# A chunk's delta-rule solve in two halves of eight tokens, with TensorE's sums between them, and all output products on GpSimd

## The chip, the cores and the metric

The kernel runs on one core of a Trainium2 chip. The metric is device microseconds (us) of one execution. The trace is of one profiled execution, with the granted TensorE clock beside it (1.0 is 2.4 GHz, 0.5 is 1.2 GHz).

## The reference, cut to what matters

Two layers, each attention plus a feed-forward part, over x of [16 batches, 512 tokens, 256]. The change touches only the recurrence of layer 0's attention. There, with 16 heads and 64 x 64 states:

```python
q = silu(conv4(x @ Wq.T)); k = silu(conv4(x @ Wk.T)) * SCALE; v = silu(conv4(x @ Wv.T))
a = sigmoid(x @ Wa.T + ba); beta = sigmoid(x @ Wb.T + bb)
def step(S, inp):                 # one token, every batch and head
    qt, kt, vt, at, bt = inp
    err = einsum('bhij,bhj->bhi', S, kt) - vt
    S = at[..., None] * S - bt[..., None, None] * (err[..., None] * kt[:, :, None, :])
    return S, einsum('bhij,bhj->bhi', S, qt)
```

## The kernel before, in words

**Work and slots.** The 512 tokens are cut into chunks of 16 (C), the 16 batches into two groups of 8. A step s is one chunk of one group: 64 steps, group s % 2. Each engine has its own program of `slot(s, ...)` for all s, and semaphores alone tie them together. In slot s, VectorE and GpSimd solve chunk s, while TensorE and ScalarE prepare chunk s+1 (projections, convolution, silu) and s+2 (gates, first two projections), and TensorE builds the update of the state that chunk s-1 leaves.

**A chunk.** `products` (L452) multiplies keys and queries of the chunk with the state before it and with the chunk's keys, ScalarE copies the sums to `prod` and writes them to `prod_dram`; the SP queue reads them back with (batch, head) pairs on the partitions, as `kp` (for the keys) and `qp` (for the queries). Each is 16 rows of 64 values and 16 dot products. The values `vb`, gates `ab` and betas `nb` come through DRAM the same way. `products` waits for all adds to the states of step s-2 (L453).

**The solve (VectorE, `solve`, L764).** `rows_bank` in PSUM holds the rows that the state gives each token's key. For token r of 16: one instruction makes the token's error times beta (`vb`, L801), then all rows behind it are multiplied by the token's gate (L807), a product of dot products and that error is formed (`t2`, L808) and added (L811). Each spans (15 - r) x 64 elements. At the end `eb`, the decays from each token to the end of the chunk, is multiplied by the errors (L818). Between the first tokens stand the state adds of the step before, `state` (L729): 8 of them, each from a bank of TensorE's.

**The outputs (GpSimd).** It scales the values by beta (L380), makes the decays `eb` one row at a time (L384) and the chunk's whole decay `acb` (L388), and then for each token multiplies the outputs' rows by the gate (L397), and adds the token's part: for tokens 3 to 10 it makes the products itself (L403, L406), for tokens 0 to 2 and 11 to 15 ScalarE makes them (`shares`, L600) and GpSimd only adds (L400).

**The state.** The finished `eb` goes to `upd_dram`, comes back as `xd` with tokens on the partitions (8 reads), TensorE forms keys times `xd` in pairs of banks (`update`, L423, 4 pairs), VectorE multiplies the state by the chunk's decay `db` (L726; `db` is `acb`, read back spread over partitions, two reads of 1 MB) and adds the banks (L736).

**Order by hand.** Order in a slot, before the change:
- VectorE: conv taps 0 to 17 (four instructions each; the norm's twelve small steps lie between taps), decay, first two state adds, solve with the other six.
- TensorE: projections 2 to 5, update pair 0, gates, pairs 1 to 3, betas, front2 (transposes of keys and values), products, projections 0 and 1 of s+2. Projections 2 and 3 share `rows_bank` and wait for the solve before.
- ScalarE: evictions and silu of the six conv banks, xnT, seeding of `rows_bank` from `kp`, gates, first shares, betas, front2 and `v_dram`, products and `prod_dram`, evictions 0 and 1 of s+2, last shares.
- SP queue (each step waits in turn): xt, upd_dram, kp, xd, db, qp, vb, ab, nb, decay_dram, o_dram.

Of the kernel before, what the change touches and what calls it, by code (L numbers as in the profile page):

```python
# [12 lines left out]
HD = H * DV  # L13
# [13 lines left out]
F1_USES, F2_USES = 4, 4  # L27
F_USES = F1_USES + F2_USES


def front1_use(s):

    return 0 if isinstance(s, int) and s == 0 else F_USES * s - F2_USES


def front2_use(s):

    return F_USES * s + (F2_USES if isinstance(s, int) and s == STEPS - 1 else F_USES)


F_BANKS = 2
CONV_BANKS = MT // 4
CONV_OPS = MT * (TAPS - 1)
VALUES_SCALED = 1
SHARED_FROM = 11
FIRST_SHARES = (0, 1, 2)
LAST_SHARES = tuple(range(SHARED_FROM, C))
SHARED = FIRST_SHARES + LAST_SHARES
SHARES = [(r, t) for r in LAST_SHARES for t in range(r, C)]

DOT_BLOCKS = ((0, 4), (4, 9), (9, 15))
SOLVE_OPS = len(DOT_BLOCKS) + C + 3 * (C - 1) + 1


def solved(r):

    return 1 + 4 * r + 1 + min(max(r - 1, 0), len(DOT_BLOCKS) - 1)


ADDS_BEFORE, ADDS_PER_ROW = 2, 2  # L60
TAP_GROUPS = CONV_BANKS * (TAPS - 1)
DECAY_OPS = C + 1


def accumulated(r):

    return DECAY_OPS + 1 + sum(2 if t in SHARED else 3 for t in range(r + 1))
# [71 lines left out]
def layer0_recurrence(nc, ins, o_dram):  # L139
# [8 lines left out]
    upd_dram = [dram(f"upd_dram{g}", [GB, H, C, DV]) for g in range(GROUPS)]  # L148
    decay_dram = [dram(f"decay_dram{g}", [2, GB * HP, DV]) for g in range(GROUPS)]
    x = ins["L0_attn_x"]  # L150

    with ExitStack() as ctx:
# [34 lines left out]
        prod = decay_or_prod[:, 0:GB * 4 * ROW].rearrange("p (b c) -> p b c", b=GB)  # L187

# [7 lines left out]
        eb = sb("eb", [128, C, DV])  # L196
        acb = sb("acb", [128, DV])
        t2 = sb("t2", [128, C - 1, DV])
        pt2 = sb("pt2", [128, C, DV])
        share = sb("share", [128, len(SHARES), DV])  # L200
# [10 lines left out]
        rows_bank = ps("rows_bank", [128, C, DV])  # L211


        def shares_of(r):
            w = C - r
            if r in LAST_SHARES:
                at_ = SHARES.index((r, r))
                return share[:, at_:at_ + w]
            return share[:, 0:w] if r == 1 else pt2[:, 0:w]

        def conv_bank(j):
            if j // 2 == 1:
                return rows_bank[:, C // 2 * (j - 2):C // 2 * (j - 1), :].rearrange("p r i -> p (r i)")
            return p_bank[j % 2][:]
# [12 lines left out]
        halo_done, bneg_done = sem("halo_done"), sem("bneg_done")  # L237
        a_wr, beta_wr, v_wr, p_wr, qp_in, kp_in, vb_in, ab_in, nb_in, upd_wr, xd_in, dec_wr, db_in, o_wr = (
# [4 lines left out]
        decayed, shares_done = sem("decayed"), sem("shares_done")  # L243
        rows_in = sem("rows_in")
        sp_passed, pool_passed, pe_passed, dve_passed = map(sem, ("sp_passed", "pool_passed", "pe_passed", "dve_passed"))

        FIRST, LOOP, LAST = -2, (4, STEPS - 5), STEPS
# [10 lines left out]
        def _(sp):  # L258
# [15 lines left out]
            def slot(s, n, g, lo, hi):  # L274
                o = 1 - g
                if valid(lo + 2, hi + 2):
                    if due(s + 2):
                        sp.wait_ge(xn_ready, s + 2)
                    held(sp, sp_passed)
                    load_x(n + 1, g)  # L280
                if updates(lo - 1, hi - 1):
                    t = s - 1
                    sp.wait_ge(solve_chain, SOLVE_OPS * (t + 1))
                    held(sp, sp_passed)
                    if due(dma_of(xd_in, n, g, -3, 16 * GB)[1]):
                        sp.wait_ge(*dma_of(xd_in, n, g, -3, 16 * GB))
                        held(sp, sp_passed)
                    sp.dma_start(upd_dram[o].rearrange("b h t i -> (b h) (t i)"), eb[:]).then_inc(upd_wr[o], 16)
                if valid(lo, hi):
                    src = prod_dram[g].rearrange("m (h k r) c -> (m h) k r c", h=4, k=2)  # L290
                    sp.wait_ge(*dma_of(p_wr, n, g, 0))
                    held(sp, sp_passed)
                    if due(SOLVE_OPS * s):
                        sp.wait_ge(solve_chain, SOLVE_OPS * s)
                        held(sp, sp_passed)
                    sp.dma_start(kp[:], src[:, 0]).then_inc(kp_in[g], 16)
# [10 lines left out]
                if updates(lo - 1, hi - 1):  # L307

                    sp.wait_ge(*dma_of(dec_wr, n, g, -1))
                    held(sp, sp_passed)  # L310
                    for par in range(2):
                        rows = decay_dram[o][par:par + 1].to_broadcast([64, GB * HP, DV])
                        sp.dma_start(db[64 * par:64 * par + 64], rows).then_inc(db_in[o], 16)
                if valid(lo, hi):
                    if due(dma_of(o_wr, n, g, -2)[1]):
                        sp.wait_ge(*dma_of(o_wr, n, g, -2))
                        held(sp, sp_passed)
                    sp.dma_start(qp[:, g], src[:, 1]).then_inc(qp_in[g], 16)
                if valid(lo + 1, hi + 1):
                    t = s + 1  # L320
                    if due(POOL_OPS * (t - 1)):
                        sp.wait_ge(pool_chain, POOL_OPS * (t - 1))
                        held(sp, sp_passed)
# [1468 lines left out]
```

## Time and profile before

| | |
|---|---|
| median of 3 runs | 7530.25 us (7524.3 to 7534.19) |
| the profiled execution | 7518.62 us, span 7516.8 us |
| busy share of the span: VectorE, TensorE, GpSimd, ScalarE | 79%, 66%, 60%, 55% |
| mean granted TensorE clock | 0.765 |
| products that end a solve (L818) | 64, median 2078 ns |
| DMA | 684.14 MB, mean 91 GB/s |

The shares are over two stages. In the page's 40 slices, VectorE is at 9 tenths in slices 2 to 23 and GpSimd in 2 to 24; in the last 16 slices layer 1 runs, with VectorE at 4 to 6. The kernel's two stages share no instruction, so the first one is to be read alone, by slots.

### The profile page before, as it was taken

How to read it: one execution, taken by the hardware profiler on the slowest of the kernel's cores; microseconds unless marked ns; L12 is line 12 of the kernel's file. 1: busy time of each engine (PE TensorE's matmuls, PEld its weight loads, DVE VectorE, ACT ScalarE, POOL GpSimd, SP SyncE). 2: the span in 40 equal slices, each digit the busy share in tenths (PEclk: the TensorE clock that was granted, in tenths of full speed). 3: DMA queues.
4: the chain of work that ended last, by engine and by line, in shares of the span. 5: the costliest groups of instructions: out<-in, count | busy, mean ns of one | idle time of the engine just before them, and what ended most of it. 6: DMA issues, size and time to landing. Idle time of an engine off the chain costs nothing. (4 is left out here: it accounts for less than half of the span.)

```text
span 7516.8 us, 144745 instructions
## 1 busy us (share of the span) xinstructions
PE 4968.9 (66%) x42311; PEld 3150.7 (42%) x42311; DVE 5944.7 (79%) x15810; ACT 4111.2 (55%) x10434; POOL 4502.3 (60%) x3976
## 2 busy tenths in 40 slices
PE   5556656565665666656666534777777777777777
PEld 3444444444444444444444422334333333433343
DVE  6999999999999999999999984556665566665665
ACT  5666666666666666666666642444444444444444
POOL 4999999999999999999999992111111111111110
PEclk7777777777677677777677766888888888888888
DMA  3545554554555455455445531111111111111111
GB/s 99 135 118 117 137 125 116 128 135 115 119 135 123 114 135 130 116 123 136 118 117 136 121 89 49 48 46 46 48 46 44 42 42 42 43 44 42 42 42 35
DMA packets 953132, 684.14 MB, mean 91 GB/s; under 512 B 836659, under 2 KB 888531, under 8 KB 938196
## 3 DMA queue, kind: packets, MB, share of 16 engines
q1 hardware_dynamic: 653524, 516.82, 28.5%
q10 hardware_dynamic: 299008, 159.92, 8.9%
q8 instruction: 303, 4.96, 0.3%
q14 instruction: 297, 2.43, 0.1%
HBM read 423.47 MB, written 253.17 MB: 90 GB/s over the span
## 5 line engine op out<-in xcount | busy, mean ns | idle before, releaser
L397 POOL TENSOR_TENSOR qp<-qp,ab 128x1024 f32<-128x1024 f32 (+15 forms) x1024 | 1411.9, 1379 | 80.4
L1154 POOL TENSOR_TENSOR ot<-ot,ln_w 128x1024 f32<-128x1024 f32 x64 | 150.6, 2354 | 1408.7 <-ACT ot L1429 1408.7
L1573 DVE TENSOR_REDUCE nmax<-w_bank 128x1 f32<-128x512 f32 x1024 | 637.8, 682 | 326.2 <-PE w_bank L1199 317.6
L718 DVE SCALAR_TENSOR_TENSOR p_bank<-y,conv_w,p_bank 128x128 f32<-128x128 f32 x3072 | 832.5, 345 | 65.9 <-ACT p_bank L549 38.5
L406 POOL TENSOR_TENSOR qp<-qp,pt 128x832 f32<-128x832 f32 (+7 forms) x512 | 810.7, 1583 | 40.1
L438 PE MATMUL d_bank<-xd,kt 32*64 32x128 f32 x7936 | 402.5, 361 | 555.1 <-DVE st L736 548.4
L504 PE MATMUL p_bank<-xnT,wqkv 128*128 128x128 f32 x4096 | 581.5, 307 | 215.4 <-ACT st L562 175.2
L504 PE MATMUL rows_bank<-xnT,wqkv 128*128 128x128 f32 x2048 | 375.6, 368 | 503.6 <-DVE eb L818 503.6
L811 DVE TENSOR_TENSOR rows_bank<-rows_bank,t 128x960 f32<-128x960 f32 (+14 forms) x960 | 671.5, 699 | 33.1
L807 DVE TENSOR_TENSOR rows_bank<-rows_bank,ab 128x960 f32<-128x960 f32 (+14 forms) x960 | 661.1, 689 | 0.0
L504 PEld LDWEIGHTS p_bank<-xnT,wqkv 128*128 128x128 f32 x4096 | 552.9, 219 | 244.9 <-issue 244.9
L808 DVE TENSOR_TENSOR t<-rows_bank,vb 128x960 f32<-128x960 f32 (+14 forms) x960 | 652.2, 679 | 0.0
L1159 POOL TENSOR_TENSOR x1b<-x,bias 128x256 f32<-128x256 f32 x64 | 46.4, 725 | 1005.4 <-DVE bst L1669 1005.4
L612 ACT ACTIVATE pt<-vb,qp 128x64 f32<-128x64 f32 x1920 | 472.2, 333 | 313.3 <-POOL qp L400 145.5
L403 POOL TENSOR_TENSOR pt<-qp,vb 128x832 f32<-128x832 f32 (+7 forms) x512 | 626.9, 1224 | 0.0
L438 PEld LDWEIGHTS d_bank<-xd,kt 32*64 32x64 f32 x7936 | 323.6, 182 | 657.2 <-issue 651.5
L504 PEld LDWEIGHTS rows_bank<-xnT,wqkv 128*128 128x128 f32 x2048 | 365.4, 281 | 513.6 <-issue 513.6
L1403 ACT ACTIVATE pt<-e_bank 128x1024 f32<-128x1024 f32 x512 | 508.0, 1019 | 105.1 <-PE e_bank L1229 102.2
L612 ACT ACTIVATE share<-vb,qp 128x64 f32<-128x64 f32 x1920 | 485.8, 338 | 112.4 <-DVE vb L801 109.4
L400 POOL TENSOR_TENSOR qp<-qp,share 128x960 f32<-128x960 f32 (+5 forms) x384 | 453.8, 1182 | 60.0 <-POOL qp L397 56.3
L466 PE MATMUL p_bank<-st 64*32 64x80 f32 x16384 | 404.9, 252 | 111.2 <-issue 89.5
L1199 PE MATMUL w_bank<-ks,qs 96*128 96x512 bf16 x1024 | 401.3, 445 | 77.3 <-DVE nmax L1573 34.0
(203 smaller groups left out, 11629.1 us busy)
## 6 DMA issues: line engine op xcount, KB each, us to landing
decay_or_prod<-decay_dram SPq DMA_DIRECT2D x124, 1024.0 KB, 11.1
prod_dram<-decay_or_prod ACTq DMA_DIRECT2D x64, 1280.0 KB, 10.4
kp<-prod_dram SPq DMA_DIRECT2D x64, 640.0 KB, 6.6
qp<-prod_dram SPq DMA_DIRECT2D x64, 640.0 KB, 14.0
a_dram<-at ACTq DMA_DIRECT2D x64, 512.0 KB
v_dram<-vt ACTq DMA_DIRECT2D x64, 512.0 KB
vb<-v_dram SPq DMA_DIRECT2D x64, 512.0 KB, 4.0
ab<-a_dram SPq DMA_DIRECT2D x64, 512.0 KB, 8.8
```

Of the source, the lines that this page charges most:

```text
L397: link(nc.gpsimd.tensor_tensor(q, q, ab[:, g, r:r + 1, :].to_broadcast([128, w, DV]), ALU.mult), 0 if shared else 1)
L403: link(nc.gpsimd.tensor_tensor(pt2[:, 0:w], qp[:, g, r:C, DV + r:DV + r + 1].to_broadcast([128, w, DV]), vb[:, g, r:r + 1, :].to_broadcast ...
L406: link(nc.gpsimd.tensor_tensor(q, q, pt2[:, 0:w], ALU.add))
L438: last[e] = nc.tensor.matmul(d_bank[e][64 * par:64 * par + 64, 128 * k:128 * k + 128], kt[32 * q:32 * q + 32, g, DK * h:DK * h + DK], xd[3 ...
L504: mm = nc.tensor.matmul(bank[:, 128 * i:128 * i + 128], wqkv[:, k, 128 * m:128 * m + 128], xnT[:, g, k, :], start=k == 0, stop=k == 1)
L612: last = nc.scalar.activation(shares_of(r)[:, t - r], vb[:, g, r, :], ACT.Copy, scale=qp[:, g, t, DV + r:DV + r + 1])
L718: nc.vector.scalar_tensor_tensor(out=zz, in0=y[:, m, :, tap:tap + C], scalar=conv_w[:, m, tap:tap + 1], in1=zz, op0=ALU.mult, op1=ALU.add) ...
L807: link(nc.vector.tensor_tensor(rows, rows, ab[:, g, r:r + 1, :].to_broadcast([128, w, DV]), ALU.mult), 1)
L808: link(nc.vector.tensor_tensor(t2[:, 0:w], column.to_broadcast([128, w, DV]), vb[:, g, r:r + 1, :].to_broadcast([128, w, DV]), ALU.mult))
L811: link(nc.vector.tensor_tensor(rows, rows, t2[:, 0:w], ALU.add))
L1403: nc.scalar.activation(pt[:, kt % 2, 2 * pr:2 * pr + 2], e_bank[pr][:], ACT.Exp, scale=float(D1) ** -0.5).then_inc(e_freed, 1)
L1573: nc.vector.tensor_reduce(nmax[:, n:n + 1], bank[:], AX.X, ALU.max, negate=True).then_inc(freed, 1)
```

## The change

- **Halves.** The solve is made of two halves of 8 tokens (`half`). In a half, rows reach only to the half's end: (7 - k) x 64 elements for its k-th token. The last three tokens with rows use one instruction a row, with a copy of the dot products in SBUF (`tail`).
- **Sums between.** What the first half's tokens give the second half's keys and queries is formed by TensorE: `scores` (dot products of the first half's keys with the second half's keys and queries, masked by batch on ScalarE into `sc`), the errors with their decays to the half's end go out (`e_dram`) and come back as `xe` (8 reads into `vt`'s tile), `cross` sums (64 matmuls), ScalarE copies them (`crossed`) to `x_dram`, and they come back as `xk`. VectorE adds its first 8 rows to `kp` at the second half's start, GpSimd its last 8 to the queries' rows.
- **GpSimd** makes all products for the outputs, scales `kp` and `qp` of the second half by the first half's decay, forms the decays of both halves at once. `shares` and `seed_rows` are gone. The values of the next step are scaled at the slot's end.
- **PSUM.** `rows_bank` is half as wide; the freed bank is the third conv bank `c_bank`, so projections wait for the silu that frees their bank, no longer for the solve.
- **Orders.** VectorE: taps 0 to 8 with the norm, first half, taps 9 to 11, decay, adds, taps 12 to 14, adds, tap 15, adds, taps 16 and 17, adds, second half. TensorE, ScalarE and SP as in the diff.

The diff, cut to its core ("..." where lines are left out):

```diff
 SP:
+                if valid(lo, hi):
+                    sp.wait_ge(solve_chain, SOLVE_OPS * s + FIRST_HALF_OPS)
...
+                    sp.dma_start(e_dram[g].rearrange("b h t i -> (b h) t i"), eb[:, 0:HALF]).then_inc(e_wr[g], 16)
...
+                    for b in range(GB):
+                        sp.dma_start(xe[C * b:C * b + HALF].rearrange("t (h i) -> t h i", h=H),
+                                     e_dram[g][b].rearrange("h t i -> t h i")).then_inc(xe_in[g], 16)
+                    sp.wait_ge(*dma_of(x_wr, n, g, 0))
...
+                    sp.dma_start(xk[:], x_dram[g].rearrange("t b h i -> (b h) t i")).then_inc(xk_in[g], 16)
+                if valid(lo + 1, hi + 1):
...
+                    sp.wait_ge(*dma_of(v_wr, n, g, 1))
...
+                    sp.dma_start(vb[:, o], v_dram[o].rearrange("t b h i -> (b h) t i")).then_inc(vb_in[o], 16)
+                    sp.wait_ge(*dma_of(p_wr, n, g, 1))
...
+                    sp.dma_start(kp[:], src[:, 0]).then_inc(kp_in[o], 16)
+                if updates(lo, hi):
+                    sp.wait_ge(solve_chain, SOLVE_OPS * (s + 1))
...
+                    sp.dma_start(upd_dram[g].rearrange("b h t i -> (b h) (t i)"), eb[:]).then_inc(upd_wr[g], 16)
+                if valid(lo + 1, hi + 1):
...
+                    sp.dma_start(qp[:, o], src[:, 1]).then_inc(qp_in[o], 16)
+                if updates(lo, hi):
...
+                    for par in range(2):
+                        rows = decay_dram[g][par:par + 1].to_broadcast([64, GB * HP, DV])
+                        sp.dma_start(db[64 * par:64 * par + 64], rows).then_inc(db_in[g], 16)
 TensorE:
+            def cross(s, n, g):
+                pe.wait_ge(*dma_of(xe_in, n, g, 0, 16 * GB))
+                for u in range(2):
+                    bank = use(cross_use(s), u)
...
+                    for k in range(HP):
+                        h = HP * u + k
+                        for q in range(4):
+                            mm = nc.tensor.matmul(bank[32 * q:32 * q + 32, DV * k:DV * k + DV],
+                                                  sc[32 * q:32 * q + 32, h % 2, h // 2, :],
+                                                  xe[32 * q:32 * q + 32, DV * h:DV * h + DV], start=True, stop=True)
...
             def slot(s, n, g, lo, hi):
...
+                if front:
+                    for j in range(2, CONV_BANKS - 1):
                         project(s + 1, 1 - g, j)
+                if state:
+                    update(*before, (0,))
+                if front:
+                    project(s + 1, 1 - g, CONV_BANKS - 1)
+                if ahead:
                     gates(s + 2, g)
                     betas(s + 2, g)
+                if valid(lo, hi):
+                    cross(s, n, g)
+                if state:
+                    update(*before, (1, 2, 3))
+                if front:
+                    scores(s + 1, 1 - g)
+                    products(s + 1, n + g, 1 - g)
                     front2(s + 1, n + g, 1 - g)
 ScalarE, slot:
+                if ahead:
                     transposed(s + 2, g)
+                    gates(s + 2, n + 1, g)
+                    betas(s + 2, n + 1, g)
+                if front:
+                    silu(s + 1, 1 - g, 3)
+                    place_keys(s + 1, 1 - g)
                 if valid(lo, hi):
+                    crossed(s, n, g, state)
+                if front:
+                    silu(s + 1, 1 - g, 4)
+                    masked_scores(s + 1, 1 - g)
+                    silu(s + 1, 1 - g, 5)
+                    products(s + 1, n + g, 1 - g)
+                    front2(s + 1, n + g, 1 - g)
 VectorE, half:
+                if later:
+                    dve.wait_ge(*dma_of(xk_in, n, g, 0))
+                    dve.wait_ge(pool_chain, POOL_OPS * s + ROWS_OPS)
+                    link(nc.vector.tensor_tensor(kp[:, t0, 0:DV], kp[:, t0, 0:DV], xk[:, 0], ALU.add), 1)
+                    link(nc.vector.tensor_tensor(rows_bank[:, 1:HALF], kp[:, t0 + 1:C, 0:DV], xk[:, 1:HALF], ALU.add), 1)
+                else:
+                    dve.wait_ge(*dma_of(kp_in, n, g, 0))
...
+                    dve.wait_ge(values_scaled, s + 1)
+                    link(nc.vector.tensor_copy(rows_bank[:, 1:HALF], kp[:, 1:HALF, 0:DV]), 1)
...
+                if later:
+                    dve.wait_ge(*dma_of(e_wr, n, g, 0))
+                    link(nc.vector.tensor_tensor(late, vb[:, g, HALF:C], late, ALU.mult), 1)
+                    link(nc.vector.tensor_tensor(early, early, acs[:, 1:2].to_broadcast([128, HALF, DV]), ALU.mult))
+                else:
...
+                    link(nc.vector.tensor_tensor(early, vb[:, g, 0:HALF], early, ALU.mult))
```

## Rows read from the trace of the kernel before

**Rows 1.** Busy time of each engine in one stretch, with clock, DMA share, GB/s
```profile
2000.00:3000.00 1000.00, 616.66 (x7374) 464.39 (x7371) 943.98 (x2304) 635.37 (x1781) 927.40 (x830) 0.71 0.54 127
```
**Rows 2.** One line: count, ns min/median/max, first and last start
```profile
L818 DVE TENSOR_TENSOR eb<-vb,eb x64: 1225/2078/2547, 135.7 to 4512.1; 128x1024 f32<-128x1024 f32 x64
```
**Rows 3.** Timeline of VectorE, one slot: start us, us, operation, count
```profile
2035.15 4.22 DVE L718 SCALAR_TENSOR_TENSOR p_bank<-y,conv_w,p_bank 128x128 f32<-128x128 f32 x16
2039.80 4.42 DVE L726 TENSOR_TENSOR st<-st,decay_or_prod 128x4096 f32<-128x4096 f32 x1 [0.42 <-DMA decay_or_prod<-decay_dram]
2044.37 1.29 DVE L736 TENSOR_TENSOR st<-d_bank,st 128x512 f32<-128x512 f32 x2
...
2047.34 0.28 DVE L801 SCALAR_TENSOR_TENSOR vb<-kp,nb,vb 128x64 f32<-128x64 f32 x1
...
2074.98 0.28 DVE L801 SCALAR_TENSOR_TENSOR vb<-rows_bank,nb,vb 128x64 f32<-128x64 f32 x1
...
2085.43 2.08 DVE L818 TENSOR_TENSOR eb<-vb,eb 128x1024 f32<-128x1024 f32 x1
```
**Rows 4.** Timeline of GpSimd, the same slot
```profile
2023.09 1.27 POOL L397 TENSOR_TENSOR qp<-qp,ab 128x512 f32<-128x512 f32 x1
...
2039.42 0.32 POOL L397 TENSOR_TENSOR qp<-qp,ab 128x64 f32<-128x64 f32 x1
2039.90 4.50 POOL L400 TENSOR_TENSOR qp<-qp,share 128x64 f32<-128x64 f32 x1 [0.16 <-POOL qp L397]
2045.27 1.90 POOL L380 TENSOR_TENSOR vb<-vb,nb 128x1024 f32<-128x1024 f32 x1 [0.87 <-POOL qp L400]
```
**Rows 5.** Timeline of SP's queue, the same slot: transfers issued
```profile
2017.72 0.36 SPq L288 DMA_DIRECT2D upd_dram<-eb  x1
...
2021.38 3.77 SPq L305 DMA_DIRECT2D xd<-upd_dram  x8
...
2026.49 0.51 SPq L318 DMA_DIRECT2D qp<-prod_dram  x1
2073.00 0.39 SPq L326 DMA_DIRECT2D vb<-v_dram  x1
```
**Rows 6.** Timeline of TensorE, this slot and the next
```profile
2031.03 1.10 PE L438 MATMUL d_bank<-xd,kt 32*64 32x128 f32 x32 [0.60 <-DMA xd<-upd_dram]
...
2087.65 6.56 PE L504 MATMUL rows_bank<-xnT,wqkv 128*128 128x128 f32 x32 [9.34 <-DVE eb L818]
...
2105.44 3.78 PE L480 MATMUL f_bank<-wa,xnT 128*128 128x512 f32 x4 [0.55 <-ACT xnT L638]
...
2116.86 1.98 PE L438 MATMUL d_bank<-xd,kt 32*64 32x128 f32 x32
```
**Rows 7.** Busy time in the stretch of the gates, columns as in rows 1
```profile
2105.00:2117.00 12.00, 11.56 (x16) 3.49 (x20) 9.42 (x19) 5.14 (x8) 10.69 (x12) 0.50 0.25 70
```
**Rows 8.** Timeline of ScalarE, end of the slot
```profile
2066.70 0.59 ACTq L589 DMA_DIRECT2D v_dram<-vt  x1
2067.41 0.77 ACT L621 ACTIVATE decay_or_prod<-p_bank 128x320 f32<-128x320 f32 x2 [0.83 <-PE p_bank L466]
...
2074.39 0.39 ACTq L627 DMA_DIRECT2D prod_dram<-decay_or_prod  x1
...
2076.56 0.25 ACT L543 ACTIVATE halo<-p_bank 128x96 f32<-128x96 f32 x1 [0.86 <-PE p_bank L504]
...
2077.36 1.48 ACT L549 ACTIVATE p_bank<-p_bank,conv_b,conv_w 128x128 f32<-128x128 f32 x4
```
**Rows 9.** The page's DMA issues: operation, count, KB each, median us to landing
```profile
prod_dram<-decay_or_prod ACTq DMA_DIRECT2D x64, 1280.0 KB, 10.4
kp<-prod_dram SPq DMA_DIRECT2D x64, 640.0 KB, 6.6
qp<-prod_dram SPq DMA_DIRECT2D x64, 640.0 KB, 14.0
...
vb<-v_dram SPq DMA_DIRECT2D x64, 512.0 KB, 4.0
```

More of the change, by code:

```diff
@@ L148, in layer0_recurrence @@
     upd_dram = [dram(f"upd_dram{g}", [GB, H, C, DV]) for g in range(GROUPS)]
+    e_dram = [dram(f"e_dram{g}", [GB, H, HALF, DV]) for g in range(GROUPS)]
+    x_dram = [dram(f"x_dram{g}", [C, GB, H, DV]) for g in range(GROUPS)]
     decay_dram = [dram(f"decay_dram{g}", [2, GB * HP, DV]) for g in range(GROUPS)]
@@ L739, in norm @@
             def norm(s, n, g, meanwhile):
[L741 removed]
+                base, made = NORM_OPS * s + 1, [0]
                 def link(ins):
@@ L762, in norm, with half @@
                 nc.vector.tensor_scalar(xn[:], xt[:], mv[:, 0:1], rs[:], ALU.subtract, ALU.mult).then_inc(xn_ready, 1)
-            def solve(s, n, g, update):
-                adds = ADDS_BEFORE
-                base, made = SOLVE_OPS * s, [0]
+            def half(s, n, g, later):
+                base, made = SOLVE_OPS * s + FIRST_HALF_OPS * later, [0]
+                t0 = HALF * later
                 def link(ins, back=0):
@@ L816, in solve @@
-                dve.wait_ge(pool_chain, POOL_OPS * s + DECAY_OPS + 1)
-                dve.wait_ge(solve_chain, base + made[0])
-                link(nc.vector.tensor_tensor(eb[:], vb[:, g], eb[:], ALU.mult))
-                assert made[0] == SOLVE_OPS
+                        continue
+                    for i in range(w):
+                        link(nc.vector.scalar_tensor_tensor(
+                            out=rows[:, i], in0=vb[:, g, r, :], scalar=tail[:, k - first + i, k - first:k - first + 1], in1=rows[:, i],
+                            op0=ALU.mult, op1=ALU.add), i)
@@ new lines, in half @@
+                assert made[0] == HALF_START[later] + TOKENS_OPS
+                early, late = eb[:, 0:HALF], eb[:, HALF:C]
+                if later:
[3 more added lines that the diff above has]
+                else:
+                    dve.wait_ge(pool_chain, POOL_OPS * s + EB_OPS)
+                    link(nc.vector.tensor_tensor(early, vb[:, g, 0:HALF], early, ALU.mult))
@@ L826, in slot, with taps, states @@
                     conv(s + 1, 1)
-                taps = iter(range(2, TAP_GROUPS))
+                ahead = iter(range(2, TAP_GROUPS // 2))
                 def more_taps():
-                    k = next(taps, None)
+                    k = next(ahead, None)
                     if k is not None and front:
                         conv(s + 1, k)
+                def taps(*ks):
+                    if front:
+                        for k in ks:
+                            conv(s + 1, k)
+                def states(p):
+                    if update:
+                        for u in range(2 * p, 2 * p + 2):
+                            state(s - 1, 1 - g, u)
                 if valid(lo + 2, hi + 2):
@@ L837, in slot @@
                     more_taps()
+                if now:
+                    half(s, n, g, 0)
+                taps(9, 10, 11)
                 if update:
                     decay(s - 1, n - 1 + g, 1 - g)
-                if update:
-                    for u in range(ADDS_BEFORE):
-                        state(s - 1, 1 - g, u)
-                if valid(lo, hi):
-                    solve(s, n, g, update)
+                states(0)
+                taps(12, 13, 14)
+                states(1)
+                taps(15)
+                states(2)
+                taps(16, 17)
+                states(3)
+                if now:
+                    half(s, n, g, 1)
             slot_loop(nc, dve, slot, FIRST, LAST, LOOP)
```

375 lines of the change are left out of this document (188 added, 187 removed).

## The prediction, made before the changed kernel ran

> **What bounds it now.** I read the slices of the span first: up to about 4530 us VectorE and GpSimd are nearly full; behind that is layer 1, which is not touched. Then the busy time of one stretch of the first part: VectorE 94%, GpSimd 93%, TensorE and ScalarE 62% and 64% [rows 1]. Then one line: the 64 products at L818 that end a chunk's solve begin between 135.7 and 4512.1 us, so a slot takes (4512.1 - 135.7) / 63 = 69.5 us [rows 2]. All that follows is about that number. VectorE's timeline of one slot shows 18 tap groups (four take 4.22) and the norm, the state's decay (4.42), four pairs of state adds (1.29 each), then 16 tokens from 2047.34 to 2085.43 [rows 3]. GpSimd runs as long beside it, and stands while VectorE's decay reads two operands in SBUF: 64 elements took 4.50 us there and 0.32 just before [rows 4]. The rest fits between: vb is asked for at 2073.00, 12 us before the solve ends; the state's update has its operand 13.3 us after the solve (upd_dram issued 2017.72, first matmul 2031.03), and VectorE adds it at 2044.37 [rows 3, 5, 6].
>
> **What VectorE no longer does.** The last eight tokens cost 2085.43 - 2074.98 = 10.45 us; all sixteen 38.1 less three pairs of state adds at 1.3 = 34.2 [rows 3]. Two halves of eight are 20.9: 13.3 saved. The three short tokens' new form (one-row sums in place of a product and a sum) I cost at nothing: as many elements, and between one instruction fewer and one more. Added: two copies or sums of 448 elements into the bank and small copies (2.1 together, by L818's 2.08 us for 1024 elements [rows 3]), three products of 512 for one of 1024 (1.0), and five of the norm's steps without a tap group beside them (0 to 0.8, they are single numbers). Net 9.4 less: 65.4 busy becomes 56, and with no new wait a slot would be about 60.
>
> **GpSimd.** Three products a token at 1.27 us for 512 elements and 0.32 and a short wait for 64 are 20 us a half, 40 for both [rows 4]. Nine decay steps (0.3 to 0.6 each, 4), three products of 512 and the values' 1.90 (6) and the stands while VectorE reads two SBUF operands (4.5 for the decay, 3 for the products of the halves) give 55 to 59. That hides in any slot of 60 and more. ScalarE loses 60 short products, which were beside the solve, and gains six copies.
>
> **What becomes late.** The next chunk's transfers and the state's update now form a ring. I go round it from T, the end of the last state add in slot s, which stands directly before the second half.
>
> 1. T to V (the next chunk's v_dram is written). TensorE's products wait for T (L453). The solve and 18 tap groups hid all behind them; the cover is now one half (13.8 with its ends) and the taps and the norm before the next half (12: nine groups at 1.06, and the norm). The new scores (64 matmuls of 32 columns, no more than two pairs' 64 of 128 columns, 2.2 to 4) run mostly before T; ScalarE then has their four copies and a silu, 2.8 after T. Eight product copies take 7.0 (2067.41 to 2074.39) [rows 8] and the start, so T + 10.9. Then front2, which is now behind the products: four banks, 4.6; v_dram is issued at T + 15.5. It took 6.3 from there until SP passed it (2066.70 to 2073.00) [rows 5, 8]; now it stands behind prod_dram, 10.4 to landing [rows 9]. Bounds 6.3 and 10; I take 6.5, since prod_dram has a start of 4.6. V = T + 22.
>
> 2. V to X (xd has landed). SP waits for V, issues vb and kp, **and only then upd_dram, qp and both parts of db**; xd comes at the start of the next slot, behind these. Before, upd, kp, xd, db and qp were issued one after another, and qp, the last, landed 14.0 after its issue at 2026.5: 23 us for the five [rows 5, 9]. kp, of the same size, lands in 6.6 [rows 9], so qp was waiting behind db, and xd will. The new row has the same five and vb (2 of its 4.0 are transfer): 24 to xd. Lower bound 15 (upd to xd as before, 13.3, and vb), upper 27. VectorE and GpSimd need only kp and vb, at V + 7.
>
> 3. X to C (the cross sums start). TensorE's list has the update's pair 0 ahead of project 5, gates, betas and the cross sums. Pair 0 takes 1.10 or 1.98; project 5 3.3 (half of 6.56) or 2.0; then ScalarE has its eviction before xnT (0.8 and 1.48), with that copy 2.8; gates 2105.44 to 2116.86, 11.4, or half of it; betas 1 or 0.5 [rows 6, 8]. At full clock 12.5, at half 21; I take 18.
>
> 4. C to the next T. Cross sums: 64 matmuls of 64 columns; the nearest row is 32 of 128 columns in 1.10 or 1.98 [rows 6], so 1.1 to 4, I take 2. Then pair 1, its adds, pair 2, adds, two tap groups, adds: with the cross sums 9.9 at full clock, 12.5 at half; I take 12.
>
> Sum: 22 + 24 + 18 + 12 = **76 us** a slot against 69.5. VectorE stands for about 18 of it: before the second pair of adds, and before the second half. That half waits after C for betas, a table load and silu, the keys, two copies (5.6), the write of x_dram (6.3, as v_dram) and its read (4.0, as vb): C + 16. It ends at C + 30, and twelve more for the taps give C + 42, where the ring's V + 7 is C + 41: nearly even, so neither lengthens it by more than 1. e_dram's way (13.3 at most, as upd to xd) is done 26 us after the first half begins, and TensorE comes to it at 35. SP's other steps (o_dram, ab, nb, xt, acb) are passed in that time.
>
> Of the clock: the gates had 0.50 for the whole 12 us in which TensorE worked on them without a pause [rows 6, 7]. The Trainium skill, "TensorE: Matmul & The Clock Gate", Part 1, says that the throttled state is the default and sustained activity releases it. By that rule pair 0 and project 5, 5 us in a row, would let the gates run in 5.7, and the ring is rival B. The row speaks against it.
>
> **Time.** 61 slots with a state's update at +6.5 are +397; the last two have none and give back about 10. 7518.6 (the profiled execution; span 7516.8) + 387 = 7906. That execution lies 11.6 us (0.15%) under the median of 7530.25, so **7915 us**.
>
> **Rivals.**
> - A, faster: xd doesn't queue behind db (bound 15 in step 2). It then lands 8 us after the first half begins, C is 22 to 26 after it, and the slot C + 42, 64 to 68 us: at 66, -3.5 x 61 - 10 = -224, **7310**, and 7250 at 65. For it: 9.4 less work on the fullest engine, and that qp's wait could be its own. Against: 14.0 beside 6.6. It decides as long as xd lands less than 12 us after the half begins; each us later is one of slot. 24%.
> - B, slower but little: full clock for pair 0, project 5 and gates, ring 71: 1.5 x 61 less 10, **7610**. For it, 5 us of work in a row; against, the rows named. 18%.
> - C, slower and much: V at 10 behind prod_dram, half clock in steps 3 and 4: 22 + 3.5 and 21 and 12.5, ring 83: **8340**. 12%.
> - D: work saved and waits added cancel within 0.25 us a slot: **7530**. 6%.
> - GpSimd as the bound would give 59, less than every case above, so it has no time of its own.
>
> The forecast has 40%; its own range is 7750 to 8150 (slots of 73.5 to 80). What can't be told from no change is about 0.2%, 15 us. Slower: 40 + 18 + 12 = 70%; same 6%; faster 24%. The range goes from A's 7250 to 8250.
>
> **What would show it.** Right: L818's successor every 76 us; the matmuls on d_bank waiting 10 us and more a slot for DMA xd; upd_dram issued behind vb and kp; VectorE near 75% busy, with its waits at the second pair of adds and at the first sum of the second half (for xk); GpSimd near 73%. Wrong: xd there before TensorE has projected bank 4; slots of 66 us; VectorE's longest wait at the first half, for kp or vb; or a half taking much more than 10.45 us for its tokens.

## The result and the profile after

The changed kernel took **7952.11 us** (median of 4 runs, 7937.91 to 7975.01) beside 7527.27 (7523.96 to 7534.19): ratio **1.057**, 95% interval 1.054 to 1.059. The forecast was 7915 us. The profiled execution has a span of 7954.9 us, at a mean granted clock of 0.748.

First the page's engine sums and three of its rows of slices:

```profile
PE 5251.1 (66%) x58695; PEld 3467.7 (44%) x58695; DVE 5439.6 (68%) x16005; ACT 3251.7 (41%) x6914; POOL 3640.6 (46%) x4232
DVE  5777777777877778777777775566656565565655
POOL 3666676666766667666666666111111111111110
PEclk7766667666676666767767676688888888888888
```

VectorE and GpSimd were at 9 tenths; now they are at 7 and 6. Nothing is full any more, and the kernel is slower: that is how a ring of waits looks. The same stretch as in [rows 1], busy time of each engine (TensorE, its weight loads, VectorE, ScalarE, GpSimd), clock, DMA share, GB/s:

```profile
2000.00:3000.00 1000.00, 605.71 (x10020) 473.64 (x10021) 752.47 (x2119) 402.14 (x898) 663.78 (x813) 0.69 0.59 135
```

VectorE fell from 94% to 75%, GpSimd from 93% to 66%. The slot's length is read from the product that ends a first half (count, ns min/median/max, first and last start), which answers to [rows 2]:

```profile
L911 DVE TENSOR_TENSOR eb<-vb,eb x64: 691/1147/1671, 119.3 to 4912.7; 128x512 f32<-128x512 f32 x64
```

(4912.7 - 119.3) / 63 = **76.1 us a slot**, against 69.5. Then the waits between 1000 and 4000 us, which are 39 slots (us in total, times, longest):

```profile
POOL qp L453 <- DMA xk<-x_dram: 738.9, 39, 22.8
DVE st L828 <- PE d_bank L493: 413.1, 82, 12.9
DVE kp L870 <- DMA xk<-x_dram: 228.6, 39, 7.1
PE d_bank L493 <- issue: 220.7, 23, 12.7
PE d_bank L493 <- DMA xd<-upd_dram: 216.1, 20, 12.5
```

VectorE stands 413.1 / 39 = 10.6 us a slot for a bank of the state's update and 5.9 for xk: the two places named ahead. TensorE stands (220.7 + 216.1) / 39 = 11.2 us a slot at pair 0, half of it booked as "issue". Why, the SP queue's timeline shows (start, us), beside [rows 5]:

```profile
2074.46 0.39 SPq L355 DMA_DIRECT2D vb<-v_dram  x1
2075.10 1.20 SPq L364 DMA_DIRECT2D kp<-prod_dram  x1
2076.59 0.34 SPq L371 DMA_DIRECT2D upd_dram<-eb  x1
2077.06 0.35 SPq L376 DMA_DIRECT2D qp<-prod_dram  x1
2077.64 1.93 SPq L383 DMA_DIRECT2D decay_or_prod<-decay_dram  x2
2083.88 11.34 SPq L305 DMA_DIRECT2D xd<-upd_dram  x8
```

upd_dram is issued behind vb and kp, then 2 MB of db (on its line `decay_or_prod`), and the eight reads of xd (64 KB each) took 11.34 us only to issue, where [rows 5] has 3.77. TensorE's timeline from pair 0 to the cross sums:

```profile
2020.56 1.98 PE L493 MATMUL d_bank<-xd,kt 32*64 32x128 f32 x32 [9.70 <-issue]
2022.47 3.78 PE L588 MATMUL c_bank<-xnT,wqkv 128*128 128x128 f32 x16
...
2028.99 2.48 PE L534 MATMUL f_bank<-wa,xnT 128*128 128x512 f32 x4 [2.31 <-ACT xnT L727]
2031.40 2.07 PE L535 MATMUL f_bank<-ba,ones 1*128 1x512 f32 x2
2033.40 3.78 PE L534 MATMUL f_bank<-wa,xnT 128*128 128x512 f32 x4
2037.12 1.12 PE L535 MATMUL f_bank<-ba,ones 1*128 1x512 f32 x2
2038.17 0.61 PE L540 MATMUL f_bank<-xnT,wbeta 128*16 128x128 f32 x4
2039.02 2.25 PE L568 MATMUL f_bank<-vt,sc 32*32 32x64 f32 x128 [0.24 <-ACT at L734]
```

### The profile page after: what moved, and what is told of

It reads as the page before. It is cut to its first block and busy times, and to the rows that moved or that the text cites. A ratio compares the mean times of both kernels' runs of the same rounds, so it can differ in the third digit from the quotient of the medians.

```text
span 7954.9 us, 175685 instructions
## 1 busy us (share of the span) xinstructions
PE 5251.1 (66%) x58695; PEld 3467.7 (44%) x58695; DVE 5439.6 (68%) x16005; ACT 3251.7 (41%) x6914; POOL 3640.6 (46%) x4232
## 5 line engine op out<-in xcount | busy, mean ns | idle before, releaser
L588 PE MATMUL p_bank<-xnT,wqkv 128*128 128x128 f32 x4096 | 708.4, 348 | 571.7 <-ACT st L652 571.7
L461 POOL TENSOR_TENSOR qp<-qp,pt 128x512 f32<-128x512 f32 (+7 forms) x1024 | 965.8, 943 | 85.4 <-issue 5.2
L456 POOL TENSOR_TENSOR qp<-qp,ab 128x512 f32<-128x512 f32 (+7 forms) x1024 | 906.9, 886 | 75.3
L458 POOL TENSOR_TENSOR pt<-qp,vb 128x512 f32<-128x512 f32 (+7 forms) x1024 | 792.6, 774 | 9.3 <-DVE vb L887 9.3
L828 DVE TENSOR_TENSOR st<-d_bank,st 128x512 f32<-128x512 f32 x496 | 320.2, 687 | 674.0 <-PE d_bank L493 661.5
L520 PEld LDWEIGHTS p_bank<-st 64*32 64x32 f32 x16384 | 443.4, 140 | 185.2 <-issue 180.4
L534 PE MATMUL f_bank<-wa,xnT 128*128 128x512 f32 x512 | 382.2, 888 | 150.7 <-ACT xnT L727 150.7
L810 DVE SCALAR_TENSOR_TENSOR c_bank<-y,conv_w,c_bank 128x128 f32<-128x128 f32 x1536 | 423.2, 350 | 3.2 <-ACT c_bank L639 3.2
L1538 ACT ACTIVATE ot<-ot,nmr,rs_b 128x64 f32<-128x64 f32 x1024 | 351.8, 431 | 98.5 <-DVE xn_b L1737 98.5
L639 ACT ACTIVATE p_bank<-p_bank,conv_b,conv_w 128x128 f32<-128x128 f32 x1024 | 377.9, 429 | 8.6
## 6 DMA issues: line engine op xcount, KB each, us to landing
decay_or_prod<-decay_dram SPq DMA_DIRECT2D x124, 1024.0 KB, 15.5
```

The lines of the kernel that those rows point to most:

```text
L456: link(nc.gpsimd.tensor_tensor(q, q, ab[:, g, r:r + 1, :].to_broadcast([128, w, DV]), ALU.mult), 1)
L458: link(nc.gpsimd.tensor_tensor(pt2[:, 0:w], qp[:, g, r:r + w, DV + r:DV + r + 1].to_broadcast([128, w, DV]), vb[:, g, r:r + 1, :].to_broad ...
L461: link(nc.gpsimd.tensor_tensor(q, q, pt2[:, 0:w], ALU.add))
L520: mm = nc.tensor.matmul(p_bank[b % 2][at_:at_ + 32, ROW * hq:ROW * hq + ROW], slot_[:, DV:DV + 2 * C], slot_[:, 0:ROW], start=True, stop=True)
L534: nc.tensor.matmul(bank[:], xnT[:, g, k, :], wa[:, k, 512 * j:512 * j + 512], start=k == 0, stop=False)
L588: mm = nc.tensor.matmul(bank[:, 128 * i:128 * i + 128], wqkv[:, k, 128 * m:128 * m + 128], xnT[:, g, k, :], start=k == 0, stop=k == 1)
```

## Experiments

Ratios are against the kernel before on the same chip. The ring is read from the timelines of the slots between 2000 and 3000 us, as means: V (v_dram written, vb issued), X (first update matmul), C (cross sums start), T (last state add), and V again. The column "whole stage" has the slot over all 64 halves, by the line of the product that ends a first half.

| kernel | median us | ratio (95%) | slot | whole stage | V to X | X to C | C to T | T to V |
| --- | --- | --- | --- | --- | --- | --- | --- | --- |
| forecast | 7915 |  | 76 |  | 24 | 18 | 12 | 22 |
| after | 7952.11 | 1.057 (1.054-1.059) | 76.5 | 76.1 | 24.3 | 17.6 | 11.2 | 23.4 |
| r1 xd first | 7823.53 | 1.039 (1.037-1.041) | 74.6 | 74.0 | 15.7 | 24.4 | 12.3 | 22.2 |
| r2 more db | 8211.72 | 1.091 (1.088-1.093) | 80.2 | 80.1 | 28.5 | 17.1 | 11.3 | 23.3 |
| r3 no cross sum | 7947.64 | 1.054 (1.051-1.056) | 78.2 | 76.4 | 25.0 | 18.6 | 11.4 | 23.2 |
| r4 gates first | 7789.75 | 1.033 (1.030-1.036) | 73.7 | 73.6 | 31.1 | 7.4 | 12.7 | 22.4 |
| r5 three moves | 7610.55 | 1.010 (1.008-1.011) | 71.4 | 71.1 | 18.4 | 17.4 | 12.4 | 23.1 |
| r6 before, products on GpSimd | 7984.57 | 1.060 (1.058-1.062) |  | 76.5 |  |  |  |  |
| r7 upd first | 7871.27 | 1.045 (1.043-1.047) | 75.6 | 74.8 | 22.4 | 18.6 | 11.3 | 23.4 |
| r8 = r5, no cross sum | 7673.01 | 1.019 (1.017-1.021) | 70.9 | 72.0 | 18.2 | 16.9 | 12.3 | 23.6 |
| r9 = r5, ab late | 7474.45 | 0.994 (0.992-0.995) | 68.7 | 68.4 | 18.5 | 14.2 | 12.2 | 23.9 |
| r10 = r9, another order on TensorE | 7531.75 | 1.001 (1.000-1.002) | 70.1 | 69.5 | 13.8 | 20.3 | 12.5 | 23.5 |
| r11 = r9, xt late | 7453.14 | 0.992 (0.989-0.995) | 68.1 | 68.1 | 18.8 | 13.6 | 11.8 | 23.8 |
| r12 = r11, values first | 7411.10 | 0.984 (0.982-0.986) | 68.0 | 67.5 | 22.6 | 13.2 | 12.1 | 20.1 |

(A window holds 11 to 14 slots, which scatter by 1.5 to 3.5 us among themselves, so a mean can lie beside the slot over the whole stage: r3 has 78.2 for 76.4, r8 70.9 for 72.0. A difference of 1 us in one term says little; the medians decide.)

**r1_xd_first**: both reads of db go from the slot's end to behind the next slot's reads of xd.

```diff
 SP, slot, behind the reads of xd:
+                if updates(lo - 1, hi - 1):
+                    sp.wait_ge(*dma_of(dec_wr, n, g, -1))
...
+                    for par in range(2):
+                        rows = decay_dram[o][par:par + 1].to_broadcast([64, GB * HP, DV])
+                        sp.dma_start(db[64 * par:64 * par + 64], rows).then_inc(db_in[o], 16)
 SP, slot's end:
-                    for par in range(2):
...
-                        sp.dma_start(db[64 * par:64 * par + 64], rows).then_inc(db_in[g], 16)
```

> The changed kernel, but SP reads db (2 MB) after xd in the next slot instead of before it. Theory R (the ring: next values written, xd landed, cross sums, last state add) says that xd waits for db in the queue: the 24.3 us from the issue of vb to the first update matmul fall by the 10 us of db's transfer less what the issue order leaves (upd_dram must land before xd is issued), to 16 to 18; the slot goes from 76.5 to 69 to 71 us and the kernel to 7500 to 7620 us. Rival Q (the round trip of the cross sums through e_dram and x_dram sets the slot, xd only comes late beside it): no change, 7900 to 8000 us. Decay may then wait for db by 1 to 2 us, which costs nothing under R.

Measured: X came 8.6 us earlier, and 6.7 us of it were lost again before C: 1.9 a slot remain, and 7823.53 us lies between the two ranges expected. So xd did stand behind db. Most of the 8.6 us is in the issue of its eight reads, 3.76 us for 11.34. What took its place is in the SP queue:

```profile
2022.75 3.76 SPq L305 DMA_DIRECT2D xd<-upd_dram  x8
2026.63 1.10 SPq L312 DMA_DIRECT2D decay_or_prod<-decay_dram  x2
2028.12 0.42 SPq L317 DMA_DIRECT2D o_dram<-qp  x1
2028.90 10.77 SPq L324 DMA_DIRECT2D ab<-a_dram  x1
2039.78 1.61 SPq L327 DMA_DIRECT2D nb<-beta_dram  x1
...
2043.72 0.35 SPq L346 DMA_DIRECT2D e_dram<-eb  x1
```

The issue of ab now holds the queue for 10.77 us, and the first half's term (e_dram) stands behind it.

**r2_db_more**: 2 MB more behind db's, into a buffer that nobody reads, and the slot's users wait for both.

```diff
+                        sp.dma_start(more_dram[g][64 * par:64 * par + 64], rows).then_inc(db_in[g], 16)
```

> The changed kernel with 2 MB more of transfer in the queue right beside db (the same rows, written to a scratch tensor in DRAM), ahead of xd. R: every us that they take comes on top of the slot: 6 to 14 us more, 8300 to 8800 us, with the first update matmul that much later after the issue of vb and the other three terms of the ring unchanged. Q, or xd passing db in the queue: under 1 us a slot, below 8020 us. Nothing of the output is changed.

Measured: xd 4.2 us later, the slot 3.7 longer (4.0 over the whole stage), the other three terms within 0.5. The direction is the one expected, the size is not: 6 to 14 us and 8300 us or more were expected, so these 2 MB cost less than that. What stands ahead of xd in its queue reaches the slot almost one to one.

**r3_no_cross_sum**: both users of xk take zeros and don't wait for it (VectorE's are shown). What the first half's tokens give the second half is left out of the result.

```diff
-                    dve.wait_ge(*dma_of(xk_in, n, g, 0))
-                    link(nc.vector.tensor_tensor(rows_bank[:, 1:HALF], kp[:, t0 + 1:C, 0:DV], xk[:, 1:HALF], ALU.add), 1)
+                    link(nc.vector.tensor_tensor(rows_bank[:, 1:HALF], kp[:, t0 + 1:C, 0:DV], zk[:, 1:HALF], ALU.add), 1)
```

> The changed kernel, with the second half taking zeros (a tile cleared once) in place of the cross sums, so that neither VectorE nor GpSimd waits for xk; all transfers, matmuls and additions stay. It leaves out what the first half's tokens give the second half. R: the second half starts 5.9 us earlier, right after the last state add, but it is not in the ring; the slot falls by 0 to 2 us, 7830 to 7955 us, and VectorE stands later instead, for vb and kp or the state pairs. Q: the slot falls by at least the 5.9 us of that wait, to below 7600 us.

Measured: no gain that this kernel's spread can tell, 7947.64 for 7952.11. The second half starts at once after T (54.9 us into the slot, for 59.3) and ends 6 us earlier (68.4 for 74.6, counted from vb's issue); that time is then stood out before the next slot. Waiting for the cross sums costs nothing while the ring is 76 us.

**r4_gates_first**: on TensorE, project 5, gates and betas ahead of pair 0.

```diff
-                    for j in range(2, CONV_BANKS - 1):
+                    for j in range(2, CONV_BANKS):
                         project(s + 1, 1 - g, j)
-                if state:
-                    update(*before, (0,))
-                if front:
-                    project(s + 1, 1 - g, CONV_BANKS - 1)
                 if ahead:
                     gates(s + 2, g)
                     betas(s + 2, g)
+                if state:
+                    update(*before, (0,))
```

> The changed kernel, but TensorE's list has project 5, gates and betas before pair 0 of the state's update, so only pair 0 and what is behind it wait for xd. R: the 17.6 us from the first update matmul to the cross sums shrink to the pair itself (2), and the start of the cross sums is set by project 5, its eviction and the gates: 24 to 27 us after the first half starts where it is 31.5 now; slot 70 to 73, 7560 to 7740 us. Q: the cross sums' own inputs and round trip are unchanged in length, but they start as much earlier, so Q too allows a gain here; it tells R from a theory in which VectorE's or GpSimd's work bounds (no change).

Measured: 2.8 us a slot; 7789.75 us misses the expected 7560 to 7740. C is now 38.5 us after vb's issue for 42.0, and the last issue for xe is at 35.1: the work between xd and the sums was 17.6 and is 7.4, and 6.8 of the gain is lost because pair 0 is reached late.

**r5_combo**: r1's move, upd_dram ahead of the wait for v_dram, and project 5 (not the gates) ahead of pair 0.

```diff
 SP, ahead of vb (moved from behind kp):
+                if updates(lo, hi):
+                    sp.wait_ge(solve_chain, SOLVE_OPS * (s + 1))
...
+                    sp.dma_start(upd_dram[g].rearrange("b h t i -> (b h) (t i)"), eb[:]).then_inc(upd_wr[g], 16)
```

> The changed kernel with three things put in another order: upd_dram issued at the solve's end, before SP waits for the next values; db after xd; TensorE's project 5 before pair 0. The first run showed that with xd in 8.6 us earlier the cross sums came only 1.9 us earlier, since e_dram and its eight reads then stood behind db. Theory R2 (the ring closes over whichever is last of gates and e_dram's way): with upd_dram out of the way xd is issued right behind vb, kp and qp, db ends before e_dram is issued, the eight reads have landed 31 to 33 us after the issue of vb, and so have the gates; the cross sums start there instead of at 42.0, the slot is 66 to 69 us and the kernel 7310 to 7500 us, faster than both. Rival: the queue's total load is the bound and any order gives what the best single step gave, 73 us and more, 7750 us and up.

Measured: 71.4 us a slot, 5.1 less than after, where 66 to 69 were expected. Still over the kernel before. The SP queue and VectorE's last product of the half, one slot:

```profile
2035.94 11.57 SPq L324 DMA_DIRECT2D ab<-a_dram  x1
...
2050.80 0.60 SPq L339 DMA_DIRECT2D decay_dram<-acb  x1
2051.65 0.38 SPq L346 DMA_DIRECT2D e_dram<-eb  x1
```
```profile
2045.29 1.20 DVE L908 TENSOR_TENSOR eb<-vb,eb 128x512 f32<-128x512 f32 x1
```

The half had ended at 2046.49; e_dram was issued 5.2 us later, behind ab. One thing more is new here: between 1000 and 4000 us, pair 0 never waits for xd (in after it stood 11.2 us a slot there). From r5 on, r10 apart, V to X no longer measures xd's way; it measures how long TensorE needs for projections 2 to 5, which now all stand ahead of pair 0.

**r7_upd_first**: only that move of upd_dram.

> The changed kernel with upd_dram alone issued before SP waits for the next values. R: its 2 us of transfer leave the queue between vb and xd, but db still stands ahead of xd, so the first update matmul comes 1 to 3 us earlier and the slot with it: 7770 to 7890 us. If it were the wait for upd_dram's landing, and not db, that holds xd, 5 us or more: below 7650 us.

Measured: 0.9 us a slot (1.9 of V to X, 1.0 lost in X to C), in the expected range.

**r8_combo_no_cross**: r5 with r3's edit.

> The kernel of the three orders with zeros in place of the cross sums, as in the third run (it leaves out what the first half's tokens give the second half). There the wait for xk was outside the ring. R2: once the cross sums start near 32, two rings are nearly of one length: the old one (cross sums, last add, values), and one through VectorE's own work (cross sums, x_dram and xk, second half, taps, first half, e_dram: 17.3 + 15.3 + 12 + 11.6 + 9.6 = 65.8). Without the wait for xk the slot falls by 1 to 3 us against the kernel of the three orders. If only the old ring counts, by nothing; if the round trip is the whole bound, by 5 and more.

Measured: not faster than r5 (7673.01 for 7610.55), where 1 to 3 us a slot less were expected. With 5 us less ring the wait for xk still isn't the bound. Why it came out slower stays open.

**r9_ab_late**: r5, with ab and nb issued behind xk.

```diff
-                    sp.dma_start(ab[:], ...)   # ahead of xt, decay_dram, e_dram
+                    sp.dma_start(ab[:], ...)   # behind xk
```

> The kernel of the three orders, with ab and nb of the next step read after xk instead of at the slot's start. In the run of the three orders e_dram was issued 5 us after the first half had ended, because the issue of ab took 11.3 us itself (1.2 before): it stood behind db's 2 MB. If that issue is what holds e_dram (theory R3), e_dram goes out within 1 us of the half's end, its reads are in at 31 us after the issue of vb, and the cross sums start at 32 to 34, where gates and betas end, instead of 35.8: slot 68 to 70 us, 7410 to 7520 us, at or a little under the kernel before. If e_dram's data wait in the queue behind db anyway, the reads land as late as before: slot 71, 7590 to 7630 us.

Measured: 68.7 us a slot, and with 0.994 (0.992 to 0.995) faster than the kernel before, by a little and as expected. But e_dram still isn't free:

```profile
2041.46 9.63 SPq L293 DMA_DIRECT2D xt<-in_L_attn_x  x1
2051.43 0.62 SPq L329 DMA_DIRECT2D decay_dram<-acb  x1
2052.41 0.36 SPq L336 DMA_DIRECT2D e_dram<-eb  x1
```

The long issue has passed to xt, the next in line.

**r10_ab_late_gates**: r9, on TensorE pair 0 between projections 4 and 5, gates and betas behind it, project 5 last, and ScalarE's eviction of that bank behind the betas. TensorE's part, against after:

```diff
                 if state:
                     update(*before, (0,))
-                if front:
-                    project(s + 1, 1 - g, CONV_BANKS - 1)
                 if ahead:
                     gates(s + 2, g)
                     betas(s + 2, g)
+                if front:
+                    project(s + 1, 1 - g, CONV_BANKS - 1)
```

> As the run beside it, and TensorE makes gates and betas before project 5, ScalarE evicts conv bank 5 after the betas. Then neither gates nor project 5 can be last before the cross sums; only e_dram's way is (31 us after the issue of vb). R3: cross sums at 31, slot 66.5 to 68.5, 7310 to 7430 us, 1.5 to 3% under the kernel before. Rival: taps 15 to 17 now wait for the late eviction and delay the last state add by as much: slot 69 to 71, no better than the run beside it.

Measured: 1.001 of before, and 57 us slower than r9 on the same chip, where 7310 to 7430 us were expected. X comes 4.7 us earlier than in r9, X to C grows by 6.1. That order cost a little.

**r11_xt_late**: r9, with xt behind xk too.

```diff
-                    load_x(n + 1 + g, o)       # ahead of decay_dram, e_dram
+                    load_x(n + 1 + g, o)       # behind nb
```

> As r9_ab_late, with the read of the attention input (xt) also moved behind xk, so that no small read stands between the state's read (db) and the write of the first half's term on SyncE. Queue theory: in r9 the issue of xt itself took 9.6 us behind db, and e_dram was issued only once it was over, about 1.3 us after the first half had ended; with xt later e_dram goes at once and the slot loses 0 to 2 us: 7350 to 7475 us. Rival: the data of e_dram waits behind db in any case, and the slot stays as in r9: 7460 to 7490 us.

Measured: 0.6 us a slot, 7453.14 us. The intervals of r9 and r11 overlap, so that this move alone gained is not shown; 7453 lies in the first expectation's range.

**r12_front2_first**: r11, with `front2` ahead of `products` on TensorE and ScalarE.

```diff
                     scores(s + 1, 1 - g)
+                    front2(s + 1, n + g, 1 - g)
                     products(s + 1, n + g, 1 - g)
-                    front2(s + 1, n + g, 1 - g)
```

> As r11_xt_late, with the value projection's tail (v_dram) ahead of the products' write (prod_dram) on TensorE and ScalarE. If what follows the last state add is bounded by prod_dram and kp, v_dram goes some 7 us earlier and prod_dram 4.5 us later, and the slot stays within 1 us of r11. If the place of v_dram behind prod_dram bounds, the slot loses 3 us or more: about 7300 us.

Measured: **7411.10 us**, ratio 0.984 (0.982 to 0.986), the fastest of all. V is 3.7 us earlier after T and X as much later after V, so the slot stays within 1 us of r11, as the first expectation has it; over the whole stage it is 67.5, r11's 68.1, so half a microsecond was won besides. Its window, its half's product, and its SP queue:

```profile
2000.00:3000.00 1000.00, 704.00 (x11462) 543.16 (x11461) 854.85 (x2386) 457.44 (x1013) 748.12 (x913) 0.71 0.67 151
```
```profile
L908 DVE TENSOR_TENSOR eb<-vb,eb x64: 691/1232/1360, 119.7 to 4374.2; 128x512 f32<-128x512 f32 x64
```
```profile
1989.10 0.34 SPq L363 DMA_DIRECT2D upd_dram<-eb  x1
1989.55 1.09 SPq L368 DMA_DIRECT2D vb<-v_dram  x1
...
2005.12 10.89 SPq L324 DMA_DIRECT2D decay_dram<-acb  x1
2018.69 0.36 SPq L331 DMA_DIRECT2D e_dram<-eb  x1
```

The long issue now falls on a write whose data is read only in the next slot, and is over before the half ends (its product ended at 2018.46): e_dram goes out 0.2 us after it. VectorE is at 85%. The first two rows show why the values ahead of the products gave so little: SP issues vb behind upd_dram, and upd_dram once the second half has ended (its last product ended at 1988.93), so V hangs on the second half here and no longer on v_dram. X hangs on TensorE's own list, in which projections 3 to 5 wait for the silu that frees their bank (us in total between 1000 and 4000 us, times, longest; 44 slots):

```profile
PE p_bank L587 <- ACT st L649: 309.0, 88, 5.5
PE c_bank L587 <- ACT z L652: 130.5, 44, 3.0
```

That is 10 us a slot.

**r6_before_all_pool**: the kernel before, with all products but the last token's on GpSimd instead of ScalarE: nearly the change's other part alone.

```diff
-SHARED_FROM = 11
-FIRST_SHARES = (0, 1, 2)
+SHARED_FROM = 15
+FIRST_SHARES = ()
```

> The kernel before with one part of the change alone: GpSimd makes the products for tokens 0 to 2 and 11 to 14, ScalarE only the last token's. GpSimd was busy 93% of the time there. Theory P (GpSimd's work is a bound of the old order): 59 more rows of products at about 2 ns an element are 7 to 8 us more, less ScalarE's waits of 1 to 2 us; slot 75 to 77 us, 7880 to 8010 us. Rival: VectorE alone bounds, under 1 us a slot, below 7590 us. Nothing of the output is changed.

Measured: 7984.57 us, as expected. The window and the line that answers to [rows 2]:

```profile
2000.00:3000.00 1000.00, 530.39 (x6718) 397.61 (x6716) 846.32 (x2069) 388.15 (x846) 941.57 (x851) 0.72 0.47 113
```
```profile
L818 DVE TENSOR_TENSOR eb<-vb,eb x64: 1225/1282/2831, 138.6 to 4955.9; 128x1024 f32<-128x1024 f32 x64
```

A slot of (4955.9 - 138.6) / 63 = 76.5, with GpSimd at 94%: 72 us of work. After has all its products on GpSimd too, and GpSimd is busy for 0.66 x 76.5 = 51 us a slot. So the halves are what makes the products affordable there, and the 76 of after and the 76 of this kernel have different reasons that happen to meet: here GpSimd is nearly full, there nothing is.

## Why the prediction was right

**The bound.** Named was a ring through v_dram, upd_dram behind vb and kp, xd behind db, the gates, and the state adds. The four terms were 24, 18, 12 and 22; they measured 24.3, 17.6, 11.2 and 23.4. Two of them were then moved in the changed kernel by edits of their own: V to X by r2 (up 4.2, slot +3.7) and by r1 and r7 (down), X to C by r4. The slot followed in part, as long as the next term did not take the gain back. r3 took the wait for xk away and nothing came of it. C to T and T to V were never moved by themselves in this ring (r12 moved T to V in a kernel where X no longer hung on V, and the slot followed by half a microsecond). That these two are links of the ring is read from the waits, not shown by a run.

**Inside the terms, some luck.** In T to V, v_dram was issued 15.6 us after T (mean of the slots in the window) for 15.5 forecast, but only because prod_dram came 1.5 later than forecast and the gap to v_dram was 1.4 shorter; vb followed 7.7 later, for 6.5. In X to C, 18 was a choice between 12.5 and 21. In V to X, the forecast had xd's data wait behind db's; in the slots shown of after and r1, 7.6 of the 8.6 us are already in the issue of its reads.

**The time** came out 37 us over the forecast (7952 for 7915), and between the profiled executions 51. The product that ends a chunk's solve in after:

```profile
L907 DVE TENSOR_TENSOR eb<-vb,eb x64: 691/837/1328, 155.6 to 4948.0; 128x512 f32<-128x512 f32 x64
```

Beside [rows 2] the first chunk ends 20 us later, the 63 slots up to the last add 416 us (6.6 each), and what is behind them 2: together the 438 us between the two spans. The forecast had 387: 61 slots at 6.5 less 10 for the end, and nothing for the first chunk.

**VectorE.** Its work was put at 56 us a slot; 0.752 x 76.5 = 57.5. It was to stand for 18 us, at the second pair of adds and for xk; it stood for 10.6 + 5.9 there. So the work fell from 65.4 by 8 us, where 9.4 were forecast.

**GpSimd** was put at 55 to 59 us (73%); it was 51 (66%). The term was too large by 4 us or more, off the path.

**The second half.** A half with its ends was put at 13.8 us. From its first sum to its last product it took 15.3, means as in the table (59.3 to 74.6), so this cost was 1.5 us too small. One of its parts is in VectorE's timeline of after:

```profile
2055.28 0.22 DVE L870 TENSOR_TENSOR kp<-kp,xk 128x64 f32<-128x64 f32 x1 [2.91 <-DMA xk<-x_dram]
2055.43 1.72 DVE L871 TENSOR_TENSOR rows_bank<-kp,xk 128x448 f32<-128x448 f32 x1
...
2083.53 0.62 DVE L877 COPY rows_bank<-kp 128x448 f32<-128x448 f32 x1
```

The sum of 448 elements with two operands in SBUF took 1.72 us, where a copy of as many took 0.62. That moved T to V (22 for 23.4) at most a little: v_dram there waits for TensorE and ScalarE, not for the half.

**The clock.** The gates were put at 11.4 us at half clock, by [rows 6, 7]. In the slot shown they took 9.2 (2028.99 to 2038.17), partly at half (3.78 and 2.07) and partly at full clock (1.12 for the same two matmuls at the end). Two stretches of it, columns as in [rows 1]:

```profile
2027.00:2030.00 3.00, 1.01 (x3) 0.54 (x4) 2.87 (x3) 2.95 (x7) 2.92 (x2) 1.00 0.35 78
2031.00:2037.00 6.00, 6.00 (x7) 1.67 (x6) 2.42 (x10) 0.60 (x1) 5.37 (x12) 0.50 0.00 0
```

The level was 0.50 while TensorE did pair 0 and project 5, 1.00 in the pause behind them, fell to 0.50 within the gates and was 1.00 again at their end. Over the 39 slots between 1000 and 4000 us the gates took 6.0 to 10.5 us, 8.5 in the mean, and 6.0 in 8 of them; in the kernel before 6.0 to 11.5, 9.0 in the mean. So the slot of [rows 6] was one of the dearest, and the single row was a poor price. The Trainium skill, "TensorE: Matmul & The Clock Gate", Part 1, has sustained activity release the throttle. By that rule, behind pair 0 and project 5, they would have taken 5.7. The trace agrees in part: the level rose as that work ended, but it fell again within the unbroken work of the gates. In r4, with the gates ahead of pair 0, one slot took 10.2 of the same mixture, the mean was 8.8. Rival B (full clock throughout) did not come; nor did C.

**Rival A** is refuted as put. Its premise, that xd doesn't wait behind db, is false (r1, r2). Its consequence too: it gave 66 us a slot once xd lands in 15. In r1 it did land in 15.7, and the slot was 74.6. The step of the working behind it, that SP passes its other steps in that time and e_dram's way is long done when TensorE comes to it, fails as soon as db stands behind xd: e_dram was issued behind the blocked issue of ab. It took r5, r9 and r11 to clear that, and 68 us was the end of it.

**What the 9 us were worth.** VectorE's work did fall, by 8 us, and in r12, which has the same instructions as after in another order, some of it arrives: 67.5 us a slot for 69.5. What still holds r12 was not isolated. After's waits for xd are gone; left on the way to X are TensorE's waits for the silus (10 us a slot, 9.2 in after, where they lay ahead of the wait for xd), and on the way to V SP's for the second half's end. VectorE's 85% leaves 10 us a slot.

## What to carry to other kernels

Halving the busiest engine's work pays only if the transfers and small sums that were hidden behind it are counted as a ring: add up the terms from one event round to itself before believing the busy sum. Look at the waits again after each move: from r5 on the old ring's first term no longer measured what it was named for. And price a step whose clock changes from many slots, not from one row. When an engine list or a queue is written by hand, look first at what stands behind the largest transfer; with every instruction kept, the order of transfers and one projection's place moved the time from 7952 to 7453 us (r11), and the values ahead of the products brought 7411. A zero in place of a suspected operand (r3) tells within one run whether a wait matters.

## What the runs showed of the hardware

**An issue soon behind 2 MB blocks, whatever it is.** With db's two reads (1 MB each) issued just before, the next transfer on the SP queue after o_dram took 10 to 11 us to *issue*, though its own data is smaller (ab 512 KB, xt 128 KB, decay_dram 32 KB). One line each of after, r1, r5, r9 and r12 (ns min/median/max):

```profile
L318 SPq DMA_DIRECT2D ab<-a_dram x64: 370/1971/3240, 38.4 to 4845.6; - x64
L333 SPq DMA_DIRECT2D decay_dram<-acb x62: 568/592/1146, 109.5 to 4775.0; - x62
```
```profile
L324 SPq DMA_DIRECT2D ab<-a_dram x64: 377/10760/11377, 35.1 to 4696.9; - x64
```
```profile
L324 SPq DMA_DIRECT2D ab<-a_dram x64: 370/11033/12553, 35.7 to 4516.8; - x64
```
```profile
L293 SPq DMA_DIRECT2D xt<-in_L_attn_x x64: 596/10105/11417, 4.1 to 4221.2; - x64
```
```profile
L324 SPq DMA_DIRECT2D decay_dram<-acb x62: 624/10683/12220, 103.1 to 4246.7; - x62
```

ab: 2.0 us in after, 10.8 and 11.0 where it stands behind db; decay_dram 0.6 and 10.7. What is issued directly behind db still passed (o_dram, 512 KB, in 0.42; in after the first four reads of xd in under 0.5 each, while the fifth took 4.4 and the eighth 3.9, medians; in r2, behind 4 MB, the fifth took 10.8). So a transfer on a queue can delay not only data behind it but the queue's engine, and every wait that this engine would have passed. Why it blocks there (how much a queue takes ahead) no run here shows.
